# Two heads in the two halves of TensorE's rows: the score matmuls of a cross-attention kernel

## The reference, cut to what matters

```python
x = x + xattn(layernorm(x), ctx)      # x (8, 256, 256), ctx (8, 1601, 256)
x = x + moe_ffn(layernorm(x))         # 8 experts, top 2, one shared expert

def xattn(ref_feat, sup_feat):
    sup = relu(sup_feat @ W_fc.T + b_fc)
    ref = relu(ref_feat @ W_fc.T + b_fc)
    q = (ref @ W_q.T + b_q)           # 16 heads of 16
    k = (sup @ W_k.T + b_k)
    p = softmax(q k.T / 4)            # per head, 256 x 1601
    attn = (p @ sup) @ Wv + b_v       # the kernel takes v = sup @ Wv first
    return ref + attn
```

## Time and profile before

| | |
|---|---|
| median of 3 runs | 1279.07 us (1276.35 to 1281.3) |
| the profiled execution | 1282.98 us |
| its span on the core | 1281.2 us |
| mean granted TensorE clock | 0.976 |
| TensorE matmul busy | 1217.5 us, 95% |
| VectorE busy | 791.7 us, 62% |
| ScalarE busy | 688.9 us, 54% |
| GpSimd busy | 371.5 us, 29% |

### The profile page before, as it was taken

One profiled execution on the slowest core, in us unless ns is written; L12 is line 12 of the kernel. 1 busy time (PEld: TensorE's weight loads), 2 busy tenths in 40 slices (PEclk: granted clock), 3 DMA queues, 4 the chain that ended last, 5 costly groups with the idle time before them and its releaser, 6 DMA issues. The chain is left out here.

```text
span 1281.2 us, 23263 instructions
## 1 busy us (share of the span) xinstructions
PE 1217.5 (95%) x8550; PEld 914.9 (71%) x8550; DVE 791.7 (62%) x1669; ACT 688.9 (54%) x954; POOL 371.5 (29%) x282
## 2 busy tenths in 40 slices
PE   6899999999999999999999999999999969999994
PEld 5767777777777777777777777766546867888884
DVE  5266676767777777777777676777835433444442
ACT  4436666666656666666666666656663222222221
POOL 4403223322332342233223222311102540223332
PEclk8879999999999999999999999999998998999998
DMA  6766576678768666776866667674615858633333
GB/s 194 228 164 178 175 209 169 184 202 214 204 220 240 182 179 206 215 198 226 229 191 175 190 177 188 197 179 93 155 59 219 327 199 279 196 56 55 51 55 90
DMA packets 164510, 228.88 MB, mean 179 GB/s; under 512 B 65568, under 2 KB 134568, under 8 KB 164336
## 3 DMA queue, kind: packets, MB, share of 16 engines
q1 hardware_dynamic: 149952, 194.80, 53.1%
q0 software_dynamic: 9216, 16.46, 6.0%
q10 hardware_dynamic: 5232, 16.13, 3.5%
HBM read 133.56 MB, written 95.68 MB: 179 GB/s over the span
## 5 line engine op out<-in xcount | busy, mean ns | idle before, releaser
L628 DVE TENSOR_REDUCE mx<-side 128x1 f32<-128x400 f32 (+1 forms) x1024 | 534.8, 569 | 143.3 <-PE side L403 134.8
L495 ACT ACTIVATE prob<-st 128x1024 f32<-128x1024 f32 (+1 forms) x416 | 412.5, 1022 | 183.6 <-PE st L424 181.7
L403 PE MATMUL side<-kst,qst 96*128 96x400 f32 (+1 forms) x1024 | 331.1, 383 | 7.0 <-DVE mx L628 3.2
L403 PEld LDWEIGHTS side<-kst,qst 96*128 96x128 f32 x1024 | 190.0, 190 | 118.8 <-issue 38.1
L424 PE MATMUL st<-qst,kst 97*128 97x512 f32 (+1 forms) x832 | 266.0, 403 | 5.3 <-ACT prob L495 3.3
L436 PE MATMUL acc<-prob,v 128*32 128x256 f32 (+1 forms) x3328 | 206.8, 384 | 0.0
L424 PEld LDWEIGHTS st<-qst,kst 97*128 97x128 f32 (+1 forms) x832 | 148.2, 186 | 18.8 <-ACT prob L495 9.0
L436 PEld LDWEIGHTS acc<-prob,v 128*32 128x32 f32 (+1 forms) x3328 | 95.4, 110 | 78.8 <-issue 21.2
L660 POOL TENSOR_TENSOR clo<-raw,chi 128x768 fp32r<-128x768 f32 (+1 forms) x32 | 60.8, 1901 | 299.1 <-ACT chi L526 299.1
L666 POOL TENSOR_TENSOR flo<-fc,fhi 128x768 fp32r<-128x768 f32 (+1 forms) x32 | 61.1, 1909 | 204.6 <-ACT fhi L539 204.6
L1550 POOL DMA_INDIRECT token_sums<-yg,rows_of x39 | 60.9, 1561 | 163.1 <-DMA token_sums<-yg,rows_of 101.6
(11 more groups left out here) (195 smaller groups left out, 1677.0 us busy)
## 6 DMA issues: line engine op xcount, KB each, us to landing
kst<-parts_at SPq DMA_DIRECT2D x90, 400.2 KB, 6.0
parts_at<-parts SPq DMA_DIRECT2D x48, 384.0 KB, 6.8
wall<-w_at ACTq DMA_DIRECT2D x10, 1536.0 KB, 9.2
w_at<-piece_hi SPq DMA_DIRECT2D x27, 512.0 KB, 6.7
w_at<-piece SPq DMA_DIRECT2D x27, 512.0 KB, 5.8
v<-v_at SPq DMA_DIRECT2D x32, 408.0 KB
raw<-ctx_t SPq DMA_DIRECT2D x24, 384.0 KB, 5.3
piece<-gate_up SPq DMA_DIRECT2D x18, 512.0 KB, 4.9
```

What stands on the lines that cost most here:

```text
L403: pe.matmul(side[u.bank][:, 0:w], t.qst[0:96, pair, col * P:(col + 1) * P], t.kst[0:96, pair, o:o + w], start=True, stop=True).then_inc(si ...
L495: act.activation(prob[0:rows, s, :], st[(KT * g + s) % 2][0:rows, :], ACT.Exp, scale=float(DH) ** -0.5).then_inc(exp_done, 1)
L628: dve.tensor_reduce(mx[:, p % 2, hq, r:r + 1], side[u.bank][:, 0:RANGES[r][1]], AX.X, ALU.max)\
```

## The change

The stacks are laid out anew. Each half of the 128 rows (`HALF = 64`) holds one head of a pair: rows 0 to 47 the three 16-row parts of the first head (`PART_ROWS = 48`) and row 48 its ones or maxima, rows 64 to 111 and row 112 the same for the second head. `qst` has 256 columns for a pair in place of 512, and no zeros. An S unit is a product over 48 rows, by turns in the upper and the lower half. The st of a step is four matmuls of 49 rows and 256 columns, by turns in the halves, where it was two of 97 rows and 512 columns; the first heads of the two pairs go to one PSUM bank and the second heads to the other. The order of the S units in `STEP` is changed so that most of them stand in twos behind an st. The key loads and the loads of ones and maxima become twice as many DMAs of half the rows. The clearing of `qst` is gone. In the expert layer ScalarE's part of the first `turn_x` comes before the issue of the three `FIRST_LATE` weight loads, where it came behind.

```diff
 STEP = [
     ["p 0", "0 xturn 0", "p 1", "1 stat"],
-    ["S", "v 0", "S", "0 xturn 1"],
-    ["S"],
-    ["S", "S", "v 1", "S", "chi", "S"],
-    ["S", "S", "1 norm", "prev 8", "prev 9", "prev 10", "prev 11", "prev 12", "accout", "S", "0 xchi"],
+    ["S", "S", "v 0", "0 xturn 1"],
+    ["S", "S"],
+    ["S", "S", "v 1", "chi", "S", "S"],
+    ["S", "S", "1 norm", "prev 8", "prev 9", "prev 10", "prev 11", "prev 12", "accout", "0 xchi"],
     ["S", "S", "f 0", "S", "S"],
-    ["S", "f 1", "S", "S"],
-    ["fhi", "S", "out", "V 0", "V 1", "S"],
+    ["S", "S", "f 1", "S"],
+    ["fhi", "S", "S", "out", "V 0", "V 1"],
     ["S", "S", "0 xfc"],
     ["S", "S"],
-    ["1 xp", "S", "1 xres", "V 2", "V 3", "V 4", "V 5", "tm", "S"],
+    ["S", "1 xp", "1 xres", "V 2", "V 3", "V 4", "V 5", "tm", "S"],
     ["S", "S"],
     ["S", "S", "V 6", "V 7", "S", "S", "S"],
 ]
...
         def pe_score(pe, u, g, n):
             bank_free(pe, u)
             r, hq = divmod(n, GQ)
             o, w = RANGES[r]
-            pair, col = GP * g + hq // 4, hq % 4
-            pe.matmul(side[u.bank][:, 0:w], t.qst[0:96, pair, col * P:(col + 1) * P], t.kst[0:96, pair, o:o + w],
-                      start=True, stop=True).then_inc(side_full, 1)
+            pair, q, at = GP * g + hq // 4, hq // 2 % QT, HALF * (hq % 2)
+            pe.matmul(side[u.bank][:, 0:w], t.qst[at:at + PART_ROWS, pair, q * P:(q + 1) * P],
+                      t.kst[at:at + PART_ROWS, pair, o:o + w], start=True, stop=True).then_inc(side_full, 1)
...
             for i in range(GP):
-                mm = pe.matmul(into[0:rows, i * 2 * NQ:(i + 1) * 2 * NQ],
-                               t.kst[0:97, GP * g + i, s * P:s * P + rows],
-                               t.qst[0:97, GP * g + i, :], start=True, stop=True)
+                for j in range(2):
+                    at, end = HALF * j, HALF * j + PART_ROWS + 1
+                    mm = pe.matmul(into[0:rows, (GP * j + i) * NQ:(GP * j + i + 1) * NQ],
+                                   t.kst[at:end, GP * g + i, s * P:s * P + rows],
+                                   t.qst[at:end, GP * g + i, :], start=True, stop=True)
             mm.then_inc(st_full, 1)
...
         def sp_load_keys(sp, b, g, o, end, s):
             pairs = slice(GP * g, GP * g + GP)
             for i, part in ((1, 1), (0, 0), (2, 0)):
-                sp.dma_start(t.kst[32 * i:32 * i + 32, pairs, o:end].bitcast(F32),
-                             rows_of(parts_at, b, part)[:, pairs, o:end]).then_inc(s, 16)
+                for j in range(2):
+                    at = HALF * j + DH * i
+                    sp.dma_start(t.kst[at:at + DH, pairs, o:end].bitcast(F32),
+                                 rows_of(parts_at, b, part)[DH * j:DH * (j + 1), pairs, o:end]).then_inc(s, 16)
...
         def sp_max_row(sp, u, g):
             unit_out(sp, u)
-            sp.dma_start(t.qst[96:97, GP * g:GP * (g + 1), :].rearrange("p a n -> p (a n)").bitcast(F32),
-                         mrow[:, :].bitcast(F32)).then_inc(row_in, 16)
+            for j in range(2):
+                at = HALF * j + PART_ROWS
+                sp.dma_start(t.qst[at:at + 1, GP * g:GP * (g + 1), :].rearrange("p a n -> p (a n)").bitcast(F32),
+                             mrow[j:GQ:2, :].bitcast(F32)).then_inc(row_in, 16)
...
-                dve.memset(t.qst[0:96, :, :].bitcast(F32), 0.0).then_inc(zero_done, 1)
...
                     shared_high(c, FT - 1)
+                turn_x(0)
...
                 for e, a in FIRST_LATE:
                     load_part(act, place(e), w_at, e, a, late_in)
-                turn_x(0)
...
-        t.qst = sb("qst", [P, PAIRS, 2 * NQ], F32R)
+        t.qst = sb("qst", [P, PAIRS, NQ], F32R)
```

More of the change, by code:

```diff
@@ L43 @@
 BANKS = 3
+HALF = P // 2
+PART_ROWS = 3 * DH
 def key_rows(kt):
@@ L297, in attention @@
         set_done = sem("set_done")
-        zero_done = sem("zero_done")
         ones_done = sem("ones_done")
@@ L393, in pe_stack_in @@
         def pe_stack_in(pe, b, g):
-            pe.wait_ge(kst_in[g], 48 * (b if g < 2 else b + 1))
+            pe.wait_ge(kst_in[g], 96 * (b if g < 2 else b + 1))
             pe.wait_ge(qst_in[g], 96 * (b + 1))
@@ L419, in pe_transposed_scores @@
             if s == 0:
-                pe.wait_ge(row_in, 16 * (p + 1))
+                pe.wait_ge(row_in, 32 * (p + 1))
             after(pe, exp_done, KT * p + s - 1)
@@ L436, in pe_values @@
                 mm = pe.matmul(acc[32 * j:32 * j + 32, 0:NQ], t.v[0:rows, g, kt, VS * j:VS * j + 32],
-                               prob[0:rows, kt, j * NQ:(j + 1) * NQ], start=(kt == 0), stop=(kt == KT - 1))
+                               prob[0:rows, kt, (GP * (j % 2) + j // 2) * NQ:(GP * (j % 2) + j // 2 + 1) * NQ],
+                               start=(kt == 0), stop=(kt == KT - 1))
             mm.then_inc(pv_done, 1)
@@ L561, in act_max_row @@
             unit_full(act, u)
-            after(act, row_in, 16 * p)
+            after(act, row_in, 32 * p)
             act.activation(mrow[:, :], side[u.bank][0:GQ, 0:P], ACT.Copy, scale=-1.0)\
@@ L789, in sp_load_queries @@
                 for j in range(2):
-                    r = 16 * j
-                    sp.dma_start(t.qst[32 * i + r:32 * i + r + 16, pairs, j * NQ:(j + 1) * NQ].bitcast(F32),
-                                 rows_of(q_at, b, part)[r:r + 16, pairs, :]).then_inc(qst_in[g], 16)
+                    at = HALF * j + DH * i
+                    sp.dma_start(t.qst[at:at + DH, pairs, :].bitcast(F32),
+                                 rows_of(q_at, b, part)[DH * j:DH * (j + 1), pairs, :]).then_inc(qst_in[g], 16)
         def sp_load_keys(sp, b, g, o, end, s):
@@ L875, in _ @@
                 sp.wait_ge(ones_done, 1)
-                sp.dma_start(t.kst[96:97, :, :].rearrange("p a n -> p (a n)").bitcast(F32), t.ones).then_inc(ones_in, 16)
+                for j in range(2):
+                    at = HALF * j + PART_ROWS
+                    sp.dma_start(t.kst[at:at + 1, :, :].rearrange("p a n -> p (a n)").bitcast(F32), t.ones)\
+                      .then_inc(ones_in, 16)
                 sp_load_chunk(sp, 1, 0, 1)
@@ L880, in _ @@
                 sp_store_queries(sp, before_unit(("xp", 0, 0)), 0)
-                sp.wait_ge(zero_done, 1)
                 sp.wait_ge(set_done, 5)
@@ L1191, in _ @@
                         if q == 0 and arg == 0:
-                            pe.wait_ge(first_in[0], 96)
+                            pe.wait_ge(first_in[0], 192)
                         if q == 0 and arg % GQ == 0 and arg // GQ + 1 < len(CHUNKS):
-                            pe.wait_ge(first_in[arg // GQ + 1], 96)
+                            pe.wait_ge(first_in[arg // GQ + 1], 192)
                         pe_score(pe, before_unit((kind, q, arg)), q, arg)
@@ L1197, in _ @@
                         pe_turn_max(pe, before_unit((kind, q, arg)), 0)
-                pe.wait_ge(ones_in, 16)
+                pe.wait_ge(ones_in, 32)
                 pe.wait_ge(set_done, 5)
```

## The result

The kernel became slower: 1342.47 us in the median of 4 runs (1336.03 to 1348.54) against 1280.18 of the kernel before in the same session (1276.35 to 1281.92), a ratio of 1.0472 (95% interval 1.0438 to 1.0507). The forecast was 1284 with a range of 1250 to 1312. The profiled execution took 1341.26 us, 58.3 more than the one before.

A forecast was written before the change was run, and what follows sets the result against it. It took TensorE's stream through 26 full phases as the bound. Against the profiled 1282.98 us, +4 +14 -8 +2 -7 = +5 gave 1288; with the median 3.9 lower, 1284, range 1250 to 1312.

The forecast's parts named there:

- the second rival: The row halves do not run together, so no matmul time is saved and the new order's waits stay: 1312, chance 0.15.
- the first rival: Changes of mode are free and the halves overlap as the V parts do: 1254, chance 0.25.
- the forecast 0.21: TensorE, 12 changes a phase between row halves and full array: 0.21 us each, for drain and late weights, as at V.
- The start-up: SP's key loads before the first phases: six more loads for each of four chunks, +4 us (0 to +8).
- Last phases ... together -8: Phases 26 to 31, without projections: shorter st and S save 8 us together (-4 to -14), VectorE binding most steps.
- 26 x 0.55 = +14: The 26 full phases: each loses 0.55 us, taken as the mean of the four groups, +14 us.
- the +2 for the maxima: The maxima's two DMAs: the second issues 0.65 us later, with slack in most phases, +2 us (0 to +6).
- the walk: One full phase timed unit by unit: 26.70 us now, 26.15 with free changes of mode, 27.38 at 0.21 each.
- one S moves ahead of `xp`: Full phases: this eases one group in four, the reason given for 0.55 us as the mean loss.
- walk 1.3 x 26 = 34: Full phases: bank waits of the new order alone, at `v 0` and `f 1`, about +1.3 us a phase, +34.
- the saved matmul time: Full phases on TensorE: halves running together save 5.7 us of st and S a phase, mostly lost to waits and changes.
- I take -7: Expert layer, `turn_x(0)` ahead of the weight loads: -7 us (-10 to -3), including 0 to +4 for the shared store.

The follow-up runs named there:

- one_half: The kernel after with every S unit and transposed-score product in the upper half of the rows, so none overlap (outputs wrong): 1401.26 us, ratio 1.0939.
- experiment 7: The kernel before with each key load cut into two DMAs of 16 rows, nothing else: 1290.25 us, ratio 1.0055.
- order_only: The kernel before with only the new order of the units; stacks, products and DMAs as before: 1309.41 us, ratio 1.0228.
- st_64_rows: The kernel before with st contracted over rows 0 to 63 alone, S units unchanged (outputs not the reference's): 1425.94 us, ratio 1.1099.
- halves_old_order: The kernel after with the old order of the units: 1320.62 us, ratio 1.0303.
- short_max_after: The kernel after with VectorE's maxima over 100 keys in place of 400 (outputs not the reference's): 1259.75, 1265.08 and 1268.38 us, ratio 0.9872.
- tail_busy: The kernel after with each st product issued three times in the last seven phases, same result: 1338.08 us, ratio 1.0449.
- Experiments 8 and 9: Maxima over 100 keys in place of 400, in the kernel before (1242.34 us, ratio 0.9692) and in the kernel after (short_max_after, ratio 0.9872).
- experiment 5: The kernel before with only ScalarE's first slot-tile transpose moved ahead of the three weight loads: 1281.52 us, ratio 0.9986.

## Why the prediction was wrong

**Right, as mechanisms.** The halves run together, so the second rival fell. Changes between row halves and full array are dear, 0.19 against the forecast 0.21, so the first rival fell too: the changes that the forecast put "on both sides" of each projection cost the 0.09 and 0.10 that it had read around V. "TensorEngine Tiling (Array Packing)", Key Properties, of the Trainium skill says that changing the mode drains TensorE; the trace agrees, and the size is 0.09 us, plus 0.10 for the weights. "TensorE: Matmul & The Clock Gate", Measured speedup vs the span model, of the Trainium skill has four row parts at 3.07 times the speed of one. The trace agrees that row parts work at once: from the first two st products to the next two it is 124 ns in the kernel after and 238 in `one_half`, 1.9 times for two parts. Banks set the new pace: `v 0` 1.58 us behind `p 1` (forecast 1.6), `f 1` 1.8 behind `f 0` (1.8). The start-up was +4.4 (+4), and experiment 7 ties it to the key loads, which alone gave 5.7.

**The step that failed first: "Last phases ... together -8".** They, phase 31 with them, took 24.6 us more. The sum has no term for the clock there: it let the shorter products shorten the phases as they would at the 1.00 of the earlier trace rows. The stretch after ran at 0.70 in phases 27 to 30, about three fifths of the time at 1.2 GHz and the rest at 2.4, with TensorE busy 96% (108.3 of 113.2 us), as before. Over phases 26 to 30 the clock of 0.73 is 78 us at half speed, worth up to 39 us (an estimate from the window's row), enough for the 26.5 lost and the 8 not gained.

Six runs separate the candidates:

```
run                 S and st                        busy   clock
order_only          full height                     95%    1.00
one_half            half height, one after another  97%    0.75
st_64_rows          only st at half height          98%    0.76
halves_old_order    half height, both halves        92%    0.80
short_max_after     the same, banks free sooner     86%    0.90
tail_busy           the same, st three times        94%    0.97
```

So the busy share doesn't tell the clock. `one_half` and `st_64_rows` have as many columns to work through as kernels at full height, and the clock falls. More half-height products in the same time bring it back. Products of half the rows hold the clock up less; in the full phases, where projections at full height stand between them, it is 0.98 to 0.99. The mechanism inside the chip is not shown. Nor is it shown that the rows alone do it: `st_64_rows` also adds 26 changes of mode a phase, and `one_half` twice as many st products of half the width.

**The second: "26 x 0.55 = +14".** It was +30.5, with the +2 for the maxima inside. For the group that I walked, the fourth, the undisturbed phases took 27.82 us by the medians of the steps:

```
steps      0-1   2-3   4     5     6-7   8-9   10-12  sum
forecast   6.04  2.92  3.59  2.08  5.21  1.51  6.03   27.38
measured   6.27  3.09  3.50  2.15  5.16  1.62  6.04   27.82
```

So the walk was 0.44 short, 0.40 of it in steps 0 to 3. Three of six phases of that group took 28.5 to 29.5: one has a wait of 1.1 us for the DMA of the maxima, and each of the other two ran at 1.2 GHz for a part of it. Taking the mean over groups lower than the walk (0.55 for 0.68), because one S moves ahead of `xp`, was wrong: by medians the first three groups lost 1.2, 0.6 and 1.2. Undisturbed phases so come to 27 us of the loss, and the rest is in the few phases with such a wait or at the low clock. The runs give the parts of the sum in place of the mean:

* order: +25.6 (walk 1.3 x 26 = 34);
* changes of mode and doubled DMAs: +50.9 (walk 1.23 x 26 = 32, and 2 for the maxima);
* running together: -45.7 (walk, by difference, 1.85 x 26 = 48).

The three measured differences add to 30.8 (by the exponentials' starts the whole is 30.9). Two of them hold waits of TensorE for the maxima's DMA: 1.8 us in `order_only`, 16.4 in `one_half`, 5.1 in the kernel after. If these count one for one, the changes cost 36 (50.9 less 14.6) against 32, running together returned 34 (45.7 less 11.3) against 48, and the maxima +3.3 against +2. They hold low clock too: TensorE ran at 1.2 GHz for 2.1 us of these phases in `order_only`, 25.7 in `one_half` and 12.9 in the kernel after. At half speed that is worth up to 12 us of the changes and up to 6 of the running together, which leaves 24 to 36 and 28 to 34. So the term that was surely mis-sized is the saved matmul time that reaches the end: 1.1 to 1.3 us a phase in place of 1.85. The pairs show it: 6.7 pairs of S a phase start together where the forecast had 14. That the order cost 8 less than the walk had it hid part of this, which is luck. Experiments 8 and 9 say where most of the rest is: behind the banks.

**The third: "I take -7" for `turn_x`.** It was -1.2. The gap closed as forecast, -9.5. The cost against it was seen (the store shares the engines with 4.6 MB) and put at 0 to +4, but it measured 8 to 9 (+8.3 here, +9.4 in experiment 5). I set the upper end too low, though the same loads had made a read of slot rows take 6.3 us in place of 2.6; the store is issued right behind them.

## What to carry to other kernels

Splitting the array's rows can pay where long runs of products are at half height; no run here shows a gain. Every step between half and full height costs about 0.19 us, as much as one 400-column product, so by the numbers of this case (an estimate) a run between two such steps must save over 0.38 us: two pairs of S, or the st of one step and a pair. Behind that, the engine which frees the banks must keep up with the doubled rate. Test an order of work alone first; here it lost as much in the full phases as the layout it served. A load moved off a critical read hits whatever comes next in the DMA engines: look for the next small transfer that an engine waits for, and put the large ones behind it, which made the one version with the kernel's own results here that beats the kernel before.

## What the runs showed that I had not expected

The granted clock can fall with TensorE busy 97 to 98%: 0.75 and 0.76 over some 150 us where S and st, or st alone, are 48, 49 or 64 rows high, against 1.00 for 96 and 97 rows at 95 to 97%. Tripling the 49-row products restored 0.97.

Rows 0 to 63 in place of 0 to 96, with the same columns, made st slower: 337 ns in place of 234 from the first product to the second, because its neighbours are of another height.
